# Turning the third norm of a decoder layer by DMA transfers, its low half split on VectorE and GpSimd

## The reference, cut to what matters

```python
x = x + attn(layernorm(x))          # 16 heads of Toeplitz form: softmax over rows, products with shifted rows
x = x + xattn(layernorm(x), ctx)    # one masked attention over a context of 512 rows
flat = layernorm(x).reshape(-1, 256)                 # the third norm
out = einsum('tnm,nmd->td', silu(flat @ wg_s) * (flat @ wu_s), wd_s)        # 2 shared experts
w, idx = top_k(softmax(flat @ router_w), 2)          # w is normalised to sum 1
out = out + sum over 16 experts of comb[e] * ((silu(flat @ wg_r[e]) * (flat @ wu_r[e])) @ wd_r[e])
x = x + out
```

## Time and profile before

| | us |
|---|---|
| three runs, median (lowest, highest) | 573.54 (573.17, 573.91) |
| the profiled execution, its own time | 573.51 |
| its span in the trace | 571.7 |
| what lies around the span | 1.8 |
| PE busy in the span | 541.9 (95%) |
| DVE, ACT, POOL busy | 426.5, 255.7, 191.8 |

### The profile page before, as it was taken

The page is one execution under the profiler, slowest core; times in us unless marked ns, Lnnn a source line. Parts: engine busy times, 40 slices in busy tenths (PEclk is TensorE's granted clock), DMA queues, the critical chain, the costliest instruction groups (busy, mean ns, idle before and its releaser), DMA issues. The chain is left out here.

```text
span 571.7 us, 12923 instructions
## 1 busy us (share of the span) xinstructions
PE 541.9 (95%) x4716; PEld 368.2 (64%) x4716; DVE 426.5 (75%) x1107; ACT 255.7 (45%) x517; POOL 191.8 (34%) x240
## 2 busy tenths in 40 slices
PE   5787889999999999999999999999999998999997
PEld 4565557566685667766786668666866675666455
DVE  5858687868885787868886888778876776677654
ACT  4565546445354254445344445434543334332332
POOL 4215150223542144223522343234421343133123
PEclk9999999999999999999999999999999999999999
DMA  8995595795439903694449743993189125300351
GB/s 256 308 367 194 182 386 180 155 322 183 112 82 251 335 17 101 148 292 151 111 100 249 242 110 77 204 310 98 51 177 325 57 74 126 64 1 1 86 102 37
DMA packets 90734, 94.70 MB, mean 166 GB/s; under 512 B 28224, under 2 KB 76224, under 8 KB 90432
## 3 DMA queue, kind: packets, MB, share of 16 engines
q1 hardware_dynamic: 90688, 94.09, 58.1%
HBM read 75.66 MB, written 12.12 MB: 154 GB/s over the span
## 5 line engine op out<-in xcount | busy, mean ns | idle before, releaser
L694 POOL TENSOR_TENSOR mid<-gated,mid 128x512 f16<-128x512 f32 x72 | 86.6, 1202 | 214.0 <-ACT mid L880 213.9
L880 ACT ACTIVATE mid<-gated 128x512 f16<-128x512 f32 x72 | 44.9, 624 | 83.3 <-DVEq L1225 80.0
L146 PE MATMUL wide<-w_d,mid 128*128 128x256 f16 x288 | 78.5, 273 | 0.0
L148 PE MATMUL wide<-w_d,mid 128*128 128x256 f16 x288 | 78.5, 273 | 0.0
L147 PE MATMUL wide<-w_d,mid 128*128 128x256 f16 x288 | 78.5, 272 | 0.0
L1203 DVE SCALAR_TENSOR_TENSOR gated<-gated,score 128x512 f32<-128x512 f32 x72 | 49.1, 682 | 37.6 <-ACT gated L875 37.5
L146 PE MATMUL rows<-h3T,w_gu 128*128 128x512 f16 x160 | 60.7, 379 | 0.3 <-DVEq L126 0.3
L146 PE MATMUL score<-h3T,w_gu 128*128 128x512 f16 x160 | 60.7, 379 | 0.2
L147 PE MATMUL rows<-h3T,w_gu 128*128 128x512 f16 x160 | 60.6, 379 | 0.0
L148 PE MATMUL rows<-h3T,w_gu 128*128 128x512 f16 x160 | 60.6, 379 | 0.0
L148 PE MATMUL score<-h3T,w_gu 128*128 128x512 f16 x160 | 60.6, 379 | 0.0
(11 more groups left out here) (249 smaller groups left out, 1402.8 us busy)
## 6 DMA issues: line engine op xcount, KB each, us to landing
toep<-z_scratch SPq DMA_DIRECT2D x14, 2048.0 KB, 18.3
stage<-comb_scratch SPq DMA_DIRECT2D x32, 512.0 KB, 8.5
toep<-z_scratch SPq DMA_DIRECT2D x4, 1024.0 KB, 11.2
x_bo<-in_x SPq DMA_DIRECT2D x8, 512.0 KB, 11.8
x_in<-in_xr SPq DMA_DIRECT2D x7, 512.0 KB, 11.1
qT<-q_scratch SPq DMA_DIRECT2D x7, 512.0 KB, 3.9
vx<-v_scratch SPq DMA_DIRECT2D x7, 512.0 KB, 5.2
out<-x_out SPq DMA_DIRECT2D x7, 512.0 KB, 3.0
```

The source lines that it names most:

```text
L146: pe.matmul(out, stationary[0], moving[0], start=start, stop=False, **kw)
L148: return pe.matmul(out, stationary[1], moving[0], start=False, stop=stop, **kw)
L694: pool.tensor_tensor(mid_slot(j, 1, late), gate_slot(j, late), mid_slot(j, 0, late), ALU.subtract).then_inc(mid_split.sem, 1)
L880: act.activation(mid_slot(j, 0, late), gate_slot(j, late), ACT.Copy).then_inc(mid_hi.sem, 1)
```

## The change

In rounds 2 to 7 the halves of the third norm are made in rows, from `h3`, and turned by two SP transfers. PE's 8 transposes, ACT's two instructions of line 784 and VectorE's two of line 1106 go in those rounds. Rounds 1 and 8 keep the old way.

- ACT writes the high half of rows 0 to 255 and of rows 256 to 511 (128 x 512 each) into the buffer `h2`, seen as fp16.
- VectorE subtracts the low half of rows 0 to 255, GpSimd that of rows 256 to 511 (128 x 512 each, two SBUF inputs).
- SP moves the high half when both parts are written, then the low half when both are subtracted, 8 blocks each.
- The turned norm goes by turns into `h3T` (odd rounds) and `cT` (even rounds).
- SP does `move_h1` ahead of `fetch_context`, and the new `move_h3` behind it.
- `logits` waits for the two transfers, and so does ACT's `take_rest` of the next round, which writes `h2`.
- Rounds 4 to 6 are written out instead of looped.

The pieces of the diff, in this order: the loop; the helpers; SP's new transfers; SP's order at the end of a round; the subtraction as GpSimd has it (VectorE's reads the same); its place in GpSimd's blocks; ACT's two places; VectorE's place; PE's wait in `logits`.

```diff
-            with eng.Fori(2 + len(CONTEXT_IN), B - 1) as it:
+            for it in range(2 + len(CONTEXT_IN), B - 1):
...
+        def h3_moved(it):
+            return 2 <= it < B
+        def h3T_of(it):
+            return h3T if it % 2 else cT
+        def h3_rows(a):
+            return h2[:].rearrange("p c e -> p (c e)").bitcast(F16).rearrange("p (a k c e) -> p a c k e", a=2, k=K2, c=C)[
+                :, a]
...
+            def move_h3(it, b):
+                if it == 2:
+                    sp.wait_ge(ctx_taken.sem, ctx_taken.at(6, UNITS))
+                sp.wait_ge(rows.ready.sem, rows.is_ready(it - 1, f"u{MID - 1}"))
+                parts_of = h2[:].rearrange("p c e -> p (c e)").bitcast(F16).rearrange("p (a n) -> p a n", a=2)
+                for a, made in enumerate((h3_hi, h3_split)):
+                    hold(sp, made, made.at(b, 2))
+                    sp.dma_start(h3T_of(it)[:, a].rearrange("p k (c s) -> p (k c) s", s=P), parts_of[:, a],
+                                 transpose=True).then_inc(h3T_moved.sem, 16)
...
+                if n and d:
+                    move_h1(it + 1)
                 if f and m:
                     fetch_context(it, it)
-                if n and d:
-                    move_h1(it + 1)
+                if h3_moved(it):
+                    move_h3(it, it - 1)
...
+            def part_h3(b, half):
+                pool.wait_ge(h3_hi.sem, h3_hi.at(b, half + 1))
+                some = slice(2 * half, 2 * half + 2)
+                pool.tensor_tensor(h3_rows(1)[:, some], h3[:, some].rearrange("p c (k e) -> p c k e", k=K2),
+                                   h3_rows(0)[:, some], ALU.subtract).then_inc(h3_split.sem, 1)
...
                 for j in range(MID):
+                    if h3_moved(it) and j == MID - 2:
+                        part_h3(it - 1, 1)
                     if d and j:
                         part_mid(it - 2, j)
...
                 for j in range(AHEAD, MID):
+                    if h3_moved(it) and j == MID - 2:
+                        part_h3(it - 1, 0)
                     if d and j < MID - 1:
                         part_mid(it - 2, j - 1)
                     if d:
                         tanh(it, it - 2, j)
+                    if h3_moved(it) and j == MID - 2:
+                        part_h3(it - 1, 1)
...
                     if m and at == C + 1:
                         normalise(it - 1, it, 2, x_res, h3, 1)
+                        if h3_moved(it):
+                            part_h3(it - 1, 0)
...
-                pe.wait_ge(turned.taken.sem, turned.is_taken(it - 1, "h3.1"))
+                if h3_moved(it - 1):
+                    pe.wait_ge(h3T_moved.sem, h3T_moved.at(it - 2, 32))
+                else:
+                    pe.wait_ge(turned.taken.sem, turned.is_taken(it - 1, "h3.1"))
```

More of the change, by code:

```diff
@@ L801, in normalise_x, with part_h3 @@
                         last.then_inc(h_ready[0].sem, 1)
+            def part_h3(b, half):
+                act.wait_ge(h_ready[2].sem, h_ready[2].at(b, half + 1))
+                some = slice(2 * half, 2 * half + 2)
+                act.activation(h3_rows(0)[:, some], h3[:, some].rearrange("p c (k e) -> p c k e", k=K2),
+                               ACT.Copy).then_inc(h3_hi.sem, 1)
             def normalise_last(b, it):
@@ L1025, in iteration @@
                         part_context_columns(5)
-                if d and m:
-                    act.wait_ge(rows.ready.sem, rows.is_ready(it, f"u{MID - 1}"))
-                if m:
-                    part_turned(it, it - 1, h3T, h3T_hi, "h3")
+                if m and not h3_moved(it):
+                    part_turned(it, 0 if it == 1 else 1, h3T_of(it), h3T_hi, "h3")
                 if first:
@@ L1090, in normalise @@
             def normalise(b, it, n, src, dst, half=0):
-                if n and not half:
+                if n == 2 and not half and h3_moved(it - 1):
+                    dve.wait_ge(h3_split.sem, h3_split.at(b, 0))
+                elif n and not half:
                     dve.wait_ge(turned.ready.sem, turned.was_ready(it, f"h{n + 1}.1"))
@@ L1827, in iteration @@
                         gate_up(it, j, some=slice(0, 1))
-                        turn_halves(it, "h3", h3, h_ready[2], it - 1)
+                        if not h3_moved(it):
+                            turn_halves(it, "h3", h3, h_ready[2], it - 1)
                         gate_up(it, j, some=slice(1, 2))
@@ L1901, in _ @@
                 iteration(it, True, True, True, True, c)
-            with pe.Fori(2 + len(CONTEXT_IN), B - 1) as it:
+            for it in range(2 + len(CONTEXT_IN), B - 1):
                 iteration(it, True, True, True, True)
```

14 lines of the change are left out of this document (12 added, 2 removed).

## The result

| | median, us | lowest to highest | profiled execution | its span |
|---|---|---|---|---|
| before | 573.80 | 573.17 to 574.33 | 573.51 | 571.7 |
| after | 571.51 | 569.42 to 572.09 | 572.09 | 570.3 |

Ratio 0.995, 95% interval 0.9936 to 0.9964: the change makes the kernel faster by 0.5%. The forecast was 573.8, no change. Its range held the time, its likeliest case did not happen. Of all executions behind this document one (628 us, a granted clock of 0.85, with SyncE's order put back) is of a slower state of the chip and is left out.

A forecast was written before the change was run, and what follows sets the result against it. PE was taken to bound the kernel. From 573.5 us, minus 5.2 for the transposes, minus 0.3 in round 7, plus 5.8 of new waits, gave 573.8 us; range 567.8 to 575.6.

The forecast's parts named there:

- its likeliest case: GpSimd gets the shared port first and PE's saving returns as waits ahead of both down products: 573.8 us, chance 0.65.
- What bounds the kernel: PE, busy 60.41 of 60.50 us a round; time is won only by taking work from PE.
- What goes: PE's 8 transposes, 0.87 us in each of six rounds, 5.2 us, plus 0.3 us of idle time in round 7.
- Step 1: VectorE's new subtraction comes 0.1 us behind GpSimd's block 7, waits for the port and ends at 339.21 in round 5.
- 5.8 us of new waits: PE waits ahead of down(8) and down(9) in six rounds, 0.92 us a round and 1.2 in round 7.
- rival B: VectorE goes first at the port, or neither engine waits; PE keeps 0.82 to 0.87 us a round: 568.1 us, chance 0.20.
- Steps 2 to 6: Port waits delay GpSimd's subtraction, VectorE's gates and GpSimd's blocks; PE waits 0.40 us before down(8), 0.52 before down(9).
- The transfers: SP's low half lands 3.2 us after GpSimd's subtraction, at 343.5 to 344.6, ahead of logits at 345.38.
- rival D: The transfers come too late for logits, landing at 347.5 and costing 2.1 us a round: 586 us, chance 0.04.
- Hidden by 0.8 to 1.9 us: The time by which the low half's transfer was to land before PE needs it for logits.
- Written-out rounds: Ending the loop over rounds 4 to 6 was put at nothing, between 0 and 0.1 us a round either way.

The follow-up runs named there:

- kernel without any turning: Changed kernel without the third norm's halves, subtractions, transfers, waits and transposes in rounds 2 to 7, part of the computation missing: 568.45 us, ratio 0.9914 to before.
- GpSimd put first: Changed kernel plus one small unread maximum on VectorE right ahead of its subtraction, so GpSimd reaches the port first: 574.91 us, ratio 1.0022 to before.
- the three with increments in the waits: Changed kernel plus 22, 27 or 33 unwaited semaphore increments where PE waits early on, shifting its instruction fetches: 570.59, 569.89 and 570.93 us.
- both runs with the small instruction: Changed kernel plus an unread maximum on VectorE, right ahead of its subtraction (574.91 us) or, as control, ahead of the norm's second half (572.96 us).

## Why the prediction was right or wrong

**What bounds the kernel: right.** PE is busy 59.44 of 59.58 us in round 5 and nothing was won or lost where PE didn't wait.

**What goes: right, if anything too low.** 0.87 to 0.91 us in rounds 3 to 5, and 1.67 in round 7 where 1.2 was forecast. About 0.4 of that is a loss that before has in round 7 alone, at PE's transposes of the second norm: VectorE's norm starts at 424.63 behind 0.63 us of idle time for GpSimd's `rstd`, where round 6 has 0.30. The forecast took round 7 for a round like the others there. What the sum lacked is round 8, where PE, once early, waits about 0.9 us at other places. The kernel without any turning does so too (60.66 for 59.65) and is 5.1 us below before.

**Step 1: wrong, and with it the sum.** The term that failed is the 5.8 us of new waits. Of its twelve PE has one, the 0.52 us ahead of the last `down(9)` (0.38 of idle time in its row), and the kernel without any turning has that one too. Rounds 3 to 5 last 66.27, 59.58 and 59.58 us for 67.14, 60.49 and 60.48. That VectorE "comes to its new subtraction 0.1 us too late" took the recorded end of the norm for the time at which VectorE's next instruction can start. It starts 0.09 us before that (337.25 for 337.34), in a tie with GpSimd (337.26), and goes first. The earlier trace rows could have told: its first row gives the norm's two instructions 0.74 us together, and they take 0.41 us each in the trace, so the second starts 0.08 us ahead of the first one's end. Instructions with a semaphore between them don't overlap (337.94 + 0.69 = 338.63, and L1209 stands at 338.66). A difference of 0.1 us between two engines was not enough to hang 5.8 us on; the chance of 0.20 for rival B was too low for what stood for it. That the tie fell to VectorE in all six rounds was in no row of before.

**Steps 2 to 6: right, under their condition.** With GpSimd put first, the chain came as written: 1.57 us on the subtraction, GpSimd's own 1.60, L1290 stretched (0.84, for the 1.0 of the forecast), waits ahead of `down(8)` and `down(9)` of 0.26 and 0.52 (forecast 0.40 and 0.52), rounds of 60.4 to 60.8 (60.5). In the changed kernel they don't arise, but for the 0.52 us ahead of `down(9)` at the start of round 8.

**The transfers: the mechanism was rival D's, which was given 0.04, and its cause stood nowhere.** The landing in 3.1 us (3.2) and the issue once GpSimd is done were as forecast. The slack from landing to `logits` was 0.50 us in round 5, since PE, 0.9 us early, wants the transfer sooner. What was missing is that one instruction packet of 0.93 us makes the landing 1.8 us later (round 6). Round 2's and 6's 2.9 us are that. "Hidden by 0.8 to 1.9 us" compared means and took no account of a single late engine.

**Written-out rounds: right for the rounds, wrong for the whole.** They bring 12 more instruction packets (37 + 21 for 29 + 17), among them the one in round 6 (before has none from 283 to 411 us). In round 2, which was written out before, the packet was there already, and what is new is that somebody waits.

**The sum as it came**, from the table of rounds: 573.5 - 6.1 (rounds 2 to 7 without their late transfers: 0.90, 0.87, 0.91, 0.90, 0.88 and 1.67) + 2.9 (the late transfers, 1.64 and 1.27) + 0.9 (round 8) + 0.9 (up to the first logits) = 572.1, the profiled execution.

## What to carry to other kernels

A tie at a shared port within 0.1 us must be forecast as two cases of about equal weight, and the engine with an instruction of its own directly ahead had the better end of it here. The slack of a transfer that an engine waits for is not safe below what one instruction packet among its own adds to the landing, 1.1 to 1.9 us here. Longer code, or any shift of it, moves such packets onto or off the transfer. Each hit was worth 0.2 to 0.3% here, so compare the rounds with and without such a packet before crediting the edit. Cutting a transfer that turns blocks doesn't make its issue cheaper: 2 blocks cost SyncE as much as 8.

## What the runs showed of the hardware that I had not expected

- An instruction packet of 16 KB takes 0.9 to 1.4 us where it met the low transfer, and that transfer then lands 4.2 to 5.0 us behind its issue in place of 3.1, with a tail at 6 to 10 GB/s after 200. That the tail is one DMA engine's share is read from its rate.
- Issuing a transfer that turns blocks takes 1.23 us on SyncE for 8 blocks and 1.28 for 2. The first packet moves 1.2 us behind the issue.
- An increment of a semaphore by TensorE, one after the other, takes 0.15 us: (20.92 - 11.14) / 64, from the first product with 128 and with 64 of them.
- Between two engines at the port: VectorE directly behind its own norm instruction went first even 0.14 us after GpSimd's recorded start (335.38 against 335.24); with a small instruction of 0.21 us in between, and the same 0.14 us (337.34 against 337.20), it did not. GpSimd came 0.22 us ahead of the norm's recorded end in the one and 0.10 in the other.
- The order of one such pair in round 8 flips between kernels that differ only elsewhere, and is worth 1.1 us each time (idle time ahead of PE's transposes of h: 1.0 us in before, after, and the three with increments in the waits; 2.1 in before written out, both runs with the small instruction, and VectorE with both halves. VectorE's second norm instruction takes 0.41 us in the first and 1.24 in the others).
